# A gated cross-attention and FP4 feed-forward layer: two ScalarE steps moved ahead of other work, and four attention products put in one PSUM bank

## The chip, the cores and the metric

The kernel runs on one core of one Trainium2 chip. The metric is the time of one execution on the device in microseconds (us), the median of several runs; lower is better. The engines are named as in the profile: PE (TensorE, the matrix multiplier; PEld is its weight load), DVE (VectorE), ACT (ScalarE), POOL (GpSimd) and SP (SyncE, which here only issues DMAs). Each engine takes its own instructions in the order in which they are written and stops at a semaphore wait until another engine has counted far enough.

## The reference

What must be computed, for x of 8 x 512 x 512 and a context of 8 x 77 x 512, all in float32:

```python
def _L0_xattn_ref(k, v, q, Wk, Wv, bv, Wq, bq, Wo, bo):
    kp = jnp.einsum('bsd,ed->bse', k, Wk)
    vp = jnp.einsum('bsd,ed->bse', v, Wv) + bv
    qp = jnp.einsum('bsd,ed->bse', q, Wq) + bq
    scores = jnp.einsum('bqd,bkd->bqk', qp, kp) * scale
    probs = jax.nn.softmax(scores, axis=-1)
    ctx = jnp.einsum('bqk,bkd->bqd', probs, vp)
    return jnp.einsum('bqd,ed->bqe', ctx, Wo) + bo

def _L0_ffn_ref(x, w_gate, w_up, w_down):
    # fp4_linear quantizes both operands in blocks of 16 to the FP4 grid, then multiplies
    gate = fp4_linear(x, w_gate)          # 512 -> 1408
    y = fp4_linear(x, w_up)
    h = jax.nn.silu(gate) * y
    return fp4_linear(h, w_down)          # 1408 -> 512

x = x + jnp.tanh(g_xattn[0]) * _L0_xattn_ref(ctx, ctx, _layernorm(x), Wk, Wv, bv, Wq, bq, Wo, bo)
x = x + jnp.tanh(g_ffn[0]) * _L0_ffn_ref(_layernorm(x), w_gate, w_up, w_down)
```

## The kernel before

**Tiling.** x is worked on in 32 tiles (NT) of 128 rows, tile t; four tiles (TILES) are one batch b. The attention of batch b is spread over the four feed-forward steps of the batch ahead of it: in step t the helper attention_part(t, at) issues the pieces of batch b = t // 4 + 1, at named places ("a1" to "a4", "mid", "soft", "d soft").

**Order.** There is no scheduler. One program for each engine is written by hand: sync_program, pool_program, scalar_program, vector_program, tensor_program. Engines meet only through semaphores. The steps up to t = 3 are written out one by one; from t = 4 they stand in a loop. What comes first on an engine holds back all that stands behind it.

**The feed-forward step of a tile.** x_stats(t) on DVE and then on POOL (L603 to L608: add epsilon, negate the mean, power -1/2, multiply) makes the factors of the layer norm. x_apply(t) on ACT (L785) writes the normed row to xwork once the POOL part is done (semaphore x_rstd). DVE finds block maxima and divides (x_scales, x_divide), ACT squares (x_squares, L720), DVE rounds (x_round, L1182 and L1184), POOL multiplies by the scale (x_times, L570), ACT and DVE split the result in two float16 parts (x_high L883, x_low L1335), and a DMA transposes them to x_T (x_turn). PE multiplies: gate_up(t, c, m) is 12 matmuls (L1658) for column chunk c of gate (m = 0) or up (m = 1), where chunks 0 and 1 have 512 columns and chunk 2 has 384. ACT applies Silu (gate_silu, L877), DVE multiplies (hidden, L1351), h goes through the same quantizing as x (h_scales, h_divide, h_squares, h_round, h_times, h_high, h_low), and down(t, g) is 33 matmuls (L1782) for a tile.

**The down weights** are prepared while tiles 0 and 1 run, in four row groups r: down_turn(r) transposes into three banks (PE, L1664), down_high(r) is three casts on ACT (L761, semaphore d_hi) that write the high part, down_subtract(r) is three matmuls on PE (L1683) that each wait for their cast, and down_low(r) casts the rest (ACT, L767). On PE, down_subtract(1) stands between the two halves gate_up(1, 1, 0) and gate_up(1, 1, 1).

**The attention of batches 1 and 2.** att_turn(b, i) on PE (L1652) transposes the normed tile i, xn_copy(b, i) on ACT (L807) copies it to xnT, and att_scores(b, i) on PE waits for that copy (xn_sb). From batch 3 (CUT) on, DMAs transpose and these copies are not there. att_values(b, i) (PE, L1746 and L1747) multiplies probabilities and values into a bank, and values(b, i) on DVE (L1307) adds the bank to x; the two alternate by semaphores att_mm and x1_made. take(bank, freed_by) on PE waits until the last reader of that bank is done. In batch 2, att_values for i = 0 and 1 stands in step 6 among the down matmuls, for i = 2 and 3 in step 7 before and behind gate_up(7, 0, 1). In batch 2 the largest key is found as well: top_turn("k") on PE, power_of("k") on DVE (L1155 to L1159), and power_spread("k") on PE (L1698), which waits for DVE.

Of the kernel before, what the change touches and what calls it, by code (L numbers as in the profile page):

```python
# [61 lines left out]
def build(nc, x, ctx_kv, g_xattn, g_ffn, Wk, Wv, bv, Wq, bq, Wo, bo, w_gate, w_up, w_down, out):  # L62
# [20 lines left out]
    with ctx:  # L83
# [38 lines left out]
        def x_tile(t):  # L122
            s = (t // TILES) % SLOTS * SLOT + t % TILES * D
            return ring[:, s:s + D]
# [49 lines left out]
        CUT = 3  # L174
# [87 lines left out]
        def down_c(r):  # L262
            if r == 0:
                return xn1[:, :, :].rearrange("p i n -> p (i n)")[:, 0:HID // 2].bitcast(BF16)
            return h_c if r % 2 == 0 else h_v[:, 0:HID // 2].bitcast(BF16)
# [19 lines left out]
        def by_k(ap, k):  # L285
            return ap.rearrange("p (k n) -> p k n", k=k)
# [7 lines left out]
        for t in range(NT):  # L294
            b, s = t // TILES + 1, t % TILES
# [15 lines left out]
        def down_bank(r, g):  # L311
            return (4, 6, 7)[(r * NG + g) % 3]
# [9 lines left out]
            return KEYS_HALF * (1 if (b + 1) * KEYS <= HALF else 2)  # L322

        def value_bank(b, i):
            return (5, 4)[i % 2] if b == 0 else (5, 7, 4, 5)[i] if b == 1 else (5, 7, 5, 7)[i] if b < CUT else (7, 5)[i % 2]

        def rest_moves():
            return sum(len(list(value_moves(b))) for b in range(STACKED, NBATCH))
# [387 lines left out]
        def scalar_program(e):  # L716
            w = Waits(e)

            def square(c, v):
                return e.activation(c, v, ACT.Square, scale=ROOT)  # L720
# [21 lines left out]
            def down_squares(r):  # L742
                w.wait_ge(d_div, r + 1)
                if r == 0:
                    w.wait_ge(xn_turned, TILES)
                else:
                    w.wait_ge(gu_turned, 20)
                if r == 3:
                    w.wait_ge(d_neg, 2)
                square(down_c(r), down_raw[:, r, :]).then_inc(d_c, 1)  # L750
# [6 lines left out]
            def down_high(r):  # L757
                for g, ks in enumerate(GROUPS):
                    w.wait_ge(d_turned, r * NG + g + 1)
                    w.wait_ge(val_mm, CT)  # L760
                    e.copy(wd_hi[:, ks[0]:ks[-1] + 1, r * P:(r + 1) * P],  # L761
                           by_k(bank[down_bank(r, g)][:, 0:len(ks) * P], len(ks))).then_inc(d_hi, 1)
# [7 lines left out]
            def ln1_apply(b):  # L770
                w.wait_ge(ln1_rstd, b + 1)
                if b > 0:
                    w.wait_ge(xn_turned, TILES * b)
                if b == 1:
                    w.wait_ge(d_neg, 1)
                if b > STACKED:
                    w.wait_ge(att_mm, TILES * b)
                for i in range(TILES):
                    e.activation(xn1[:, i, :], x_tile(b * TILES + i), ACT.Identity, bias=shift1[:, i:i + 1], scale=rstd1[:, i:i + 1]).then_inc(xn_made, 1)

            def x_apply(t):
                w.wait_ge(x_rstd, t + 1)
                if t > 0:
                    w.wait_ge(xq_made, t)
                e.activation(x_v, x_tile(t), ACT.Identity, bias=shift2[:, :], scale=rstd2[:, :]).then_inc(x_norm, 1)  # L785
# [34 lines left out]
            def xn_apply(b, i):  # L820
                m = cut_tile(b, i)
                w.wait_ge(ln1_rstd, b + 1)
                if m >= 2:
                    w.wait_ge(xn_lo, m - 1)
                else:
                    w.wait_ge(xn_turned, TILES * CUT)
                    w.wait_ge(k_parts, KD)
                e.activation(xn1[:, 2 + i % 2, :], x_tile(b * TILES + i), ACT.Identity, bias=shift1[:, i:i + 1], scale=rstd1[:, i:i + 1]).then_inc(xn_made, 1)

            def xn_high(b, i):  # L830
                m = cut_tile(b, i)
                w.wait_ge(xn_made, b * TILES + i + 1)
                if i < 2:
                    w.wait_ge(att_mm, TILES * b)
                else:
                    w.wait_ge(*xn_there(b, i - 2))
                e.copy(xn_parts[i % 2][:, 0:D], xn1[:, 2 + i % 2, :]).then_inc(xn_hi, 1)

            def key_high(k):
                w.wait_ge(pow_ready, NTH["k"])  # L840
                w.wait_ge(xn_turned, TILES * CUT)
                w.wait_ge(v_stacked, VALUES_MOVED * (CUT - STACKED))
                if k == 3:
                    w.wait_ge(k_parts, 1)
                e.activation(key_work[k][:, 0:CUT_COLS], key_rest(k), ACT.Copy, scale=k_scale[:, :]).then_inc(k_hi, 1)

            def key_back(k):
                w.wait_ge(k_lo, k + 1)
                e.copy(key_rest(k).bitcast(F16).rearrange("p (b h n) -> p b h n", h=2, n=KEYS),
                       key_work[k].rearrange("p (h b n) -> p b h n", h=2, n=KEYS)).then_inc(k_parts, 1)  # L850
# [40 lines left out]
            def attention_part(t, at):  # L891
                b, s = t // TILES + 1, t % TILES
                if b >= NBATCH:
                    return
                if b == CUT - 1 and (s, at) == (2, "d soft"):
                    key_high(0)
                    key_high(1)
                elif b == CUT - 1 and (s, at) == (3, "a2"):
                    key_back(0)
                    key_back(1)  # L900
                    key_high(2)
                    key_high(3)
                elif b == CUT - 1 and (s, at) == (3, "a3"):
                    key_back(2)
                    key_back(3)
                elif b >= CUT and (s, at) == (0, "d apply"):
                    xn_apply(b, 0)
                    xn_apply(b, 1)
                    xn_high(b, 0)
                    xn_high(b, 1)  # L910
                elif b >= CUT and (s, at) == (1, "a1"):
                    xn_apply(b, 2)
                    xn_apply(b, 3)
                    xn_high(b, 2)
                    xn_high(b, 3)
                elif b >= CUT and (s, at) in ((0, "a3"), (0, "a4"), (1, "a2")):
                    return
                elif (s, at) == (0, "d apply"):
                    ln1_apply(b)
                elif (s, at) == (0, "a3"):  # L920
                    xn_copy(b, 0)
                elif (s, at) == (0, "a4"):
                    xn_copy(b, 1)
                elif (s, at) == (1, "a1"):
                    xn_copy(b, 2)
                elif (s, at) == (1, "a2"):
                    xn_copy(b, 3)
                elif (s, at) == (1, "d apply") and b >= STACKED:
                    value_high(b)
                elif (s, at) == (1, "d soft"):  # L930
                    exps(b)
                    if b >= STACKED:
                        prob_high(b)
                elif (s, at) == (2, "a1") and b < STACKED:
                    prob_copy(b)
# [113 lines left out]
            attention_part(1, "a1")  # L1049
            attention_part(1, "a2")  # L1050
            down_squares(3)
            down_high(1)
            x_apply(3)
            gate_silu(1, 1)
            down_low(1)
            down_high(2)
# [30 lines left out]
            for t in range(4, NT):  # L1087
                if t == 4:
                    h_squares(t - 1, 1)
                    gate_silu(t, 0)  # L1090
                    x_apply(t + 1)
                    h_high(t - 1, 0)
                    x_squares(t + 1)
                    x_high(t + 1)
                    gate_silu(t, 1)
                    h_high(t - 1, 1)
                else:
                    h_squares(t - 1, 1)
                    gate_silu(t, 0)
                    attention_part(t, "a1")  # L1100
                    h_high(t - 1, 0)
                    attention_part(t, "a2")
                    if t + 1 < NT:
                        x_squares(t + 1)
                    gate_silu(t, 1)
                    h_high(t - 1, 1)
                    if t % TILES == 0:
                        attention_part(t, "d apply")
                    if t + 1 < NT:
                        x_high(t + 1)  # L1110
                if t % TILES != 0 or t == 4:
                    attention_part(t, "d apply")
                gate_silu(t, 2)
                attention_part(t, "a3")
                h_squares(t, 0)
                attention_part(t, "a4")
                if t + 2 < NT:
                    x_apply(t + 2)
                attention_part(t, "d soft")
            h_squares(NT - 1, 1)  # L1120
            h_high(NT - 1, 0)
# [933 lines left out]
```

## Time and profile before

| | |
|---|---|
| Runs of the kernel before | 845.83, 843.76, 845.54 us; median 845.54 us |
| The profiled execution | 845.83 us, of which the span from the first to the last instruction is 844.0 us |
| Around the span | 1.8 us |
| Busy: PE, DVE | 834.8 us, 706.1 us |
| Busy: POOL, ACT | 400.5 us, 377.3 us |
| Granted clock of PE, mean | 0.997 of full |

The profile is of one execution. Timeline rows give the start in us from the span's start, the time of the instruction (or of several in a row, with xcount), engine, line and operation; in brackets stands how long the engine sat idle before it and what ended that. A matmul's time overlaps the next one's, so on PE the pace is read from start to start. The granted clock is 1.00 at 2.4 GHz and 0.50 at 1.2 GHz.

### The profile page before, as it was taken

To read this page: it belongs to the slowest core of one execution; us is meant where nothing else is said; L and a number is where in the kernel's file an instruction comes from. 1 tells how busy PE (TensorE), PEld (TensorE's weight loads), DVE (VectorE), ACT (ScalarE), POOL (GpSimd) and SP (SyncE) were. 2 spreads that over 40 slices of the span, in tenths; PEclk is the share of its full clock that TensorE was granted. 3 is DMA by queue.
4 is the path that set the end of the run, shared out by engine and by line. 5 is a ranking of instruction groups with operands and counts; after the bars stand their busy time and mean duration, and the time that the engine had idled before them with its cause. 6 is when DMAs were issued, how large, how long until landed. Compare 5 with 4: busy or idle time off the path is not lost.

```text
span 844.0 us, 11581 instructions
## 1 busy us (share of the span) xinstructions
PE 834.8 (99%) x4175; PEld 426.1 (50%) x4175; DVE 706.1 (84%) x1094; ACT 377.3 (45%) x669; POOL 400.5 (47%) x364
## 2 busy tenths in 40 slices
PE   9999999999998999999999999999999999999998
PEld 5566556544554445444544444445544454444443
DVE  5997989898989889888888888888897998877753
ACT  2666485643544544434453445335532454333320
POOL 4496437355544354446434544445354444444321
PEclk9999999999999999999999999999999999999999
DMA  9723020054324215432452254324432343222332
GB/s 317 278 70 118 18 61 14 14 119 109 72 59 122 60 28 116 114 68 55 104 134 60 60 110 97 96 60 85 87 81 59 71 93 77 54 57 51 62 63 72
DMA packets 170527, 72.69 MB, mean 86 GB/s; under 512 B 154227, under 2 KB 155621, under 8 KB 170471
## 3 DMA queue, kind: packets, MB, share of 16 engines
q1 hardware_dynamic: 170471, 71.97, 35.8%
q8 instruction: 33, 0.54, 0.3%
q14 instruction: 23, 0.19, 0.1%
HBM read 22.76 MB, written 8.39 MB: 37 GB/s over the span
## 4 chain that ended last, share of the span: by engine, by line
PE 62%; DVE 4%; issue 3%; POOL 1%; ACT 1%; DMA 1%; SPq 0%; POOLq 0%; ACTq 0%; DVEq 0%
PE banks L1658 39%; PE banks L1782 20%; PE banks L1721 1%; PE banks L1747 1%; PE banks L1746 1%; DVE arena L1182 1%; DVE arena L1184 1%; POOL arena L570 0%; DMA arena<-h_parts 0%; DMA x_T<-x_parts 0%; POOL rstd L597 0%; PE banks L1722 0%; DVE x_parts L1335 0%; DVE stats L1224 0%; DVE h_s L1131 0%
## 5 line engine op out<-in xcount | busy, mean ns | idle before, releaser
L1658 PE MATMUL banks<-wgu_hi,x_T 128*128 128x512 f16 (+1 forms) x1536 | 442.4, 362 | 0.1
L1658 PE MATMUL banks<-wgu_lo,x_T 128*128 128x512 f16 (+1 forms) x768 | 278.1, 362 | 0.0
L1782 PE MATMUL banks<-wd,arena 128*128 128x512 f16 x1056 | 233.8, 379 | 0.5 <-DMA arena<-h_parts 0.5
L1658 PEld LDWEIGHTS banks<-wgu_hi,x_T 128*128 128x128 f16 x1536 | 150.5, 98 | 154.7 <-issue 2.6
L1782 PEld LDWEIGHTS banks<-wd,arena 128*128 128x128 f16 x1056 | 102.9, 98 | 122.1 <-issue 0.9
L570 POOL TENSOR_TENSOR arena<-arena,h_r 128x1024 f32<-128x1024 f32 (+1 forms) x60 | 91.1, 1519 | 127.3 <-DVE h_r L1136 127.3
L570 POOL TENSOR_TENSOR arena<-arena,h_s 128x1024 f32<-128x1024 f32 x64 | 90.3, 1411 | 63.2 <-DVE arena L1184 45.2
L1658 PEld LDWEIGHTS banks<-wgu_lo,x_T 128*128 128x128 f16 x768 | 75.3, 98 | 76.8 <-issue 1.8
L570 POOL TENSOR_TENSOR xwork<-xwork,x_s 128x512 f32<-128x512 f32 x32 | 34.2, 1069 | 154.9 <-DVE xwork L1184 154.7
L1351 DVE SCALAR_TENSOR_TENSOR arena<-arena,scal,banks 128x512 f32<-128x512 f32 (+1 forms) x90 | 62.1, 690 | 34.6 <-PE banks L1658 30.5
L1182 DVE SCALAR_TENSOR_TENSOR arena<-arena 128x384 f32<-128x384 bf16 (+1 forms) x67 | 70.9, 1059 | 17.9 <-ACT arena L720 17.8
L877 ACT ACTIVATE arena<-banks,scal 128x512 f32<-128x512 f32 (+1 forms) x96 | 61.8, 644 | 49.8 <-PE banks L1658 49.7
L720 ACT ACTIVATE arena<-arena 128x384 bf16<-128x384 f32 (+1 forms) x67 | 54.2, 809 | 60.7 <-POOL arena L570 60.5
L785 ACT ACTIVATE xwork<-ring,shift,rstd 128x512 f32<-128x512 f32 x32 | 26.1, 814 | 120.4 <-POOL shift L608 120.4
L1184 DVE SCALAR_TENSOR_TENSOR arena<-arena 128x384 f32<-128x384 bf16 (+1 forms) x67 | 67.6, 1008 | 2.3
L570 POOL TENSOR_TENSOR arena<-arena,valo 128x1024 f32<-128x1024 f32 x22 | 49.4, 2263 | 29.5 <-DVE valo L1136 19.3
L1370 DVE TENSOR_TENSOR h_parts<-arena,h_parts 128x1024 f16<-128x1024 f32 x64 | 60.6, 950 | 2.1 <-ACT h_parts L889 2.0
L889 ACT CAST h_parts<-arena 128x1024 f16<-128x1024 f32 x64 | 49.2, 771 | 14.6 <-POOL arena L570 14.6
L1131 DVE TENSOR_REDUCE h_s<-arena 128x64 f32<-128x1024 f32 (+1 forms) x60 | 52.7, 878 | 0.5
L720 ACT ACTIVATE xwork<-xwork 128x512 bf16<-128x512 f32 x32 | 20.1, 628 | 61.7 <-DVE xwork L1327 61.7
L1375 DVE SCALAR_TENSOR_TENSOR ring<-banks,scal,ring 128x512 f32<-128x512 f32 x32 | 23.8, 744 | 28.5 <-PE banks L1782 28.4
L883 ACT CAST x_parts<-xwork 128x512 f16<-128x512 f32 x32 | 19.7, 617 | 44.4 <-POOL xwork L570 44.4
(175 smaller groups left out, 1009.1 us busy)
## 6 DMA issues: line engine op xcount, KB each, us to landing
ring<-in_x_dram SPq DMA_DIRECT2D x8, 1024.0 KB, 5.2
out_dram<-ring SPq DMA_DIRECT2D x32, 256.0 KB, 2.0
arena<-in_L_ffn_w_down_dram SPq DMA_DIRECT2D x4, 704.0 KB, 4.0
arena<-in_L_ffn_w_gate_dram SPq DMA_DIRECT2D x5, 512.0 KB, 9.7
arena<-in_L_ffn_w_up_dram SPq DMA_DIRECT2D x5, 512.0 KB, 10.4
ring<-in_L_xattn_Wk_dram SPq DMA_DIRECT2D x4, 256.0 KB, 6.2
ring<-in_L_xattn_Wq_dram SPq DMA_DIRECT2D x4, 256.0 KB, 6.8
wd<-in_ctx_dram SPq DMA_DIRECT2D x1, 1024.0 KB
```

Of the source, the lines that this page charges most:

```text
L570: return e.tensor_tensor(blocks(dst), blocks(src), spread(s), ALU.mult)
L720: return e.activation(c, v, ACT.Square, scale=ROOT)
L785: e.activation(x_v, x_tile(t), ACT.Identity, bias=shift2[:, :], scale=rstd2[:, :]).then_inc(x_norm, 1)
L877: e.activation(silu[par][:, 0:n], bank[par][:, 0:n], ACT.Silu, scale=p_gu).then_inc(silu_done, 1)
L889: e.copy(h_parts[:, PARTS[i]], h_q[:, PARTS[i]]).then_inc(h_hi[i], 1)
L1131: e.tensor_reduce(s, blocks(src), axis=AX_X, op=ALU.max, apply_absolute_value=True).then_inc(*step())
L1182: e.scalar_tensor_tensor(between, square, FLOOR, v, ALU.add, ALU.add).then_inc(*step())
L1184: return e.scalar_tensor_tensor(v, square, FLOOR, between, ALU.add, ALU.subtract)
L1351: e.scalar_tensor_tensor(h_of(t)[:, c0:c0 + n], silu[par][:, 0:n], h_fold, bank[2 + par][:, 0:n], ALU.mult, ALU.mult).then_inc(h_made, 1)
L1370: e.tensor_tensor(h_parts[:, lo], h_q[:, PARTS[i]], h_parts[:, PARTS[i]], ALU.subtract).then_inc(h_lo[i], 1)
L1658: ended = e.matmul(at, l, r, start=(i == 0), stop=(i == len(terms) - 1))
L1782: ended = e.matmul(down_ps(t)[:, :], l, r, start=(k == 0 and i == 0), stop=(k == KH - 1 and i == 2))
```

## The change

```diff
@@ value_bank: the PSUM bank of att_values(b, i) and values(b, i)
-            return (5, 4)[i % 2] if b == 0 else (5, 7, 4, 5)[i] if b == 1 else (5, 7, 5, 7)[i] if b < CUT else (7, 5)[i % 2]
+            return (5, 4)[i % 2] if b == 0 else (5, 7, 4, 5)[i] if b == 1 else 5 if b < CUT else (7, 5)[i % 2]
@@ scalar_program, written-out part
             attention_part(1, "a1")
             attention_part(1, "a2")
             down_squares(3)
+            x_apply(3)
             down_high(1)
-            x_apply(3)
             gate_silu(1, 1)
             down_low(1)
             down_high(2)
@@ scalar_program, loop for t in range(4, NT)
                 gate_silu(t, 2)
                 attention_part(t, "a3")
                 h_squares(t, 0)
-                attention_part(t, "a4")
                 if t + 2 < NT:
                     x_apply(t + 2)
+                attention_part(t, "a4")
                 attention_part(t, "d soft")
```

First, x_apply(3) stands before the three casts of down_high(1) instead of behind them. On ACT, in the written-out part (L785 is x_apply(3), the L761 rows are down_high(1), the L877 row is gate_silu(1, 1)):

```order
 L807 COPY xnT<-banks 128x512 [waits score_mm,xn_turned] x2
 L720 ACTIVATE arena<-arena 128x1408 [waits d_neg,d_div]
+L785 ACTIVATE xwork<-ring,shift,rstd 128x512 [waits x_rstd]
 L761 CAST wd<-banks 128x4x128 [waits d_turned] x2
 L761 CAST wd<-banks 128x3x128 [waits d_turned]
-L785 ACTIVATE xwork<-ring,shift,rstd 128x512 [waits x_rstd]
 L877 ACTIVATE arena<-banks,scal 128x512 [waits h_made,gate_mm]
 L767 CAST wd<-banks 128x4x128 [waits d_less] x2
```

The wait for x_rstd now stands ahead of the casts, and the casts behind it.

Second, in the loop x_apply(t + 2) stands before attention_part(t, "a4"). ACT has something at "a4" only for batch 2, which is t = 4, so that one pair changes places. On ACT at the end of step 4 (L785 is x_apply(6), the moved L807 is xn_copy(2, 1), the L796 and L720 rows are h_squares(4, 0) and (4, 1)):

```order
 L796 ACTIVATE h_s<-h_s 128x64 [waits h_rec0]
 L720 ACTIVATE arena<-arena 128x1024 [waits h_rounded0,h_div0]
+L785 ACTIVATE xwork<-ring,shift,rstd 128x512 [waits x_rstd]
 L807 COPY xnT<-banks 128x512 [waits score_mm,xn_turned]
-L785 ACTIVATE xwork<-ring,shift,rstd 128x512 [waits x_rstd]
 L796 ACTIVATE h_s<-h_s 128x24 [waits h_rec1]
 L720 ACTIVATE arena<-arena 128x384 [waits h_rounded1,h_div1]
```

The copy that att_scores(2, 1) waits for now stands behind a wait for POOL.

Third, the four products of batch 2 all go to bank 5 instead of banks 5, 7, 5, 7. On PE the order is the same, only waits differ. In step 6, among the down matmuls (L1782), at att_values(2, 1):

```order
 L1782 MATMUL banks<-wd,arena 128x512 [waits h_turned,x2_made]
 L1782 MATMUL banks<-wd,arena 128x512 x23
-L1746 MATMUL banks<-valo,xn 128x512 [waits pow_ready]
+L1746 MATMUL banks<-valo,xn 128x512 [waits x1_made]
 L1747 MATMUL banks<-valo,xn 128x512
 L1782 MATMUL banks<-wd,arena 128x512 x9
```

Each of the products i = 1, 2, 3 now waits (x1_made) until DVE has done values(2, i - 1), where before i = 2 waited for values(2, 0) and i = 3 for values(2, 1). DVE, POOL and SP have the same instructions in the same order.

## Rows read from the trace of the kernel before

**Rows 1.** The page, part 1: busy us, share of the span, instructions.

```profile
PE 834.8 (99%) x4175; PEld 426.1 (50%) x4175; DVE 706.1 (84%) x1094; ACT 377.3 (45%) x669; POOL 400.5 (47%) x364
```

**Rows 2.** Windows: stretch, length, busy of each engine, PE's clock, DMA share, GB/s.

```profile
250.00:270.00 20.00, 17.84 (x83) 8.60 (x82) 17.11 (x38) 11.11 (x20) 6.32 (x5) 0.91 0.41 108
...
290.00:330.00 40.00, 39.85 (x207) 19.16 (x206) 35.34 (x59) 19.22 (x34) 20.68 (x21) 1.00 0.42 88
```

**Rows 3.** Timeline of ACT around down_high(1), x_apply(3) and gate_silu(1, 1).

```profile
136.72 1.46 ACT L761 CAST wd<-banks 128x512 f16<-128x512 f32 x3 [0.23 <-PE banks L1664]
140.43 0.81 ACT L785 ACTIVATE xwork<-ring,shift,rstd 128x512 f32<-128x512 f32 x1 [2.26 <-POOL shift L608]
141.15 0.67 ACT L877 ACTIVATE arena<-banks,scal 128x512 f32<-128x512 f32 x1
```

**Rows 4.** Timeline of PE at down_subtract(1) and what follows it.

```profile
139.88 0.76 PE L1683 MATMUL banks<-wd,neg_ident 128*128 128x512 f16 x3
140.47 0.38 PE L1658 MATMUL banks<-wgu_hi,x_T 128*128 128x512 f16 x1
```

**Rows 5.** Timeline of POOL: first and last of x_stats(2), then of x_stats(3).

```profile
119.12 0.23 POOL L603 TENSOR_SCALAR mv<-mv 128x1 f32<-128x1 f32 x1
...
120.37 0.19 POOL L608 TENSOR_TENSOR shift<-shift,rstd 128x1 f32<-128x1 f32 x1
...
135.16 0.55 POOL L603 TENSOR_SCALAR mv<-mv 128x1 f32<-128x1 f32 x1
...
139.32 1.08 POOL L608 TENSOR_TENSOR shift<-shift,rstd 128x1 f32<-128x1 f32 x1
```

**Rows 6.** Timelines: down_turn(3) on PE, down_high(3) on ACT, h_round(0, 0) on DVE.

```profile
149.60 1.36 PE L1664 MATMUL banks<-ident,arena 128*128 128x128 f32 x11
...
150.24 1.46 ACT L761 CAST wd<-banks 128x512 f16<-128x512 f32 x3 [1.06 <-PE banks L1664]
...
155.24 1.22 DVE L1182 SCALAR_TENSOR_TENSOR arena<-arena 128x1024 f32<-128x1024 bf16 x1 [1.84 <-ACT arena L720]
```

**Rows 7.** Timeline of ACT: xn_copy(2, 1), x_apply(6), xn_copy(2, 3), x_squares(6).

```profile
223.94 0.59 ACT L807 COPY xnT<-banks 128x512 f32<-128x512 f32 x1 [0.33 <-PE banks L1652]
227.66 0.81 ACT L785 ACTIVATE xwork<-ring,shift,rstd 128x512 f32<-128x512 f32 x1 [3.13 <-POOL shift L608]
...
231.80 0.59 ACT L807 COPY xnT<-banks 128x512 f32<-128x512 f32 x1 [0.81 <-PE banks L1652]
...
234.68 0.63 ACT L720 ACTIVATE xwork<-xwork 128x512 bf16<-128x512 f32 x1 [1.42 <-DVE xwork L1327]
```

**Rows 8.** Timeline of PE: att_scores(2, 1), then top_turn("v").

```profile
226.33 1.01 PE L1658 MATMUL banks<-keyq,xnT 128*128 128x77 f32 x8
...
230.21 0.23 PE L1691 MATMUL banks<-ident,scal 77*1 77x77 f32 x1
```

**Rows 9.** Timeline of DVE: power_of("v") and x_round(6).

```profile
233.48 0.22 DVE L1155 TENSOR_REDUCE scal<-banks 1x1 f32<-1x77 f32 x1
...
235.72 0.67 DVE L1182 SCALAR_TENSOR_TENSOR xwork<-xwork 128x512 f32<-128x512 bf16 x1
```

**Rows 10.** Timeline of PE at power_spread("k").

```profile
259.27 0.49 PE L1698 MATMUL banks<-scal,ones 1*128 1x1 f32 x2 [2.16 <-DVE scal L1159]
```

**Rows 11.** The chain that ended last, in order of time: start, us, what.

```profile
259.76 5.50 PE banks L1658 x24
...
265.69 5.18 PE banks L1782 x24
...
278.87 0.22 PE banks L1746
...
313.73 3.17 DMA x_T<-x_parts
...
323.19 9.08 PE banks L1658 x48
```

**Rows 12.** Timeline of DVE: values(2, 2).

```profile
278.38 0.65 DVE L1307 SCALAR_TENSOR_TENSOR ring<-banks,rden,ring 128x512 f32<-128x512 f32 x1
```

## The prediction

> **What bounds the kernel now.** I read the page's busy times first. PE is busy 99% of the span [rows 1], so what the change can win or lose is time in which PE stands still or runs at the lower clock. The timeline of PE and the windows show where that is. Between the start-up and the tail there is one stretch that matters: at 257 to 263 us. PE was done at 257.1 and waited 2.16 us for DVE's largest key before power_spread("k") at 259.27 [rows 10]. Behind that wait the granted clock fell: over 250 to 270 it averages 0.91 [rows 2], and 24 matmuls of 384 columns took 5.50 us in the chain. At full clock 24 of 512 and 24 of 384 columns take 9.08 us together and 24 of 512 take 5.18, so 24 of 384 take 3.90 [rows 11]. The fall to 1.2 GHz cost 5.50 - 3.90 = 1.6 us. After that PE idles 0.15 us in 290 to 330 [rows 2], where it waits for the transposed x_T whose DMA starts at 313.73 [rows 11]. From there to the tail PE does not stop. So up to about 317 us PE and the loop of DVE, ACT and POOL run neck and neck, and whatever delay is there at 317 stays in the time to the end. Nothing in the change touches the code behind that.
>
> **Edit 1: x_apply(3) ahead of down_high(1).** Before, the three casts of down_high(1) ran on ACT at 136.72 for 1.46 us, then ACT idled 2.26 us until POOL's factors let x_apply(3) start at 140.43, and gate_silu followed at 141.15, 0.72 later [rows 3]. POOL's instructions do not change, so x_apply(3) still starts at 140.43: nothing is won on it, and its reader on DVE comes only after 150 us. The casts now start where the silu started, at 141.15, and end at 141.15 + 1.46 = 142.6. PE wants them at 139.88, for down_subtract(1) [rows 4]. Its three matmuls each wait for a cast; the last can start at about 142.65 and takes 0.2. The next gate_up matmul, 140.47 before [rows 4], starts at about 142.9. **Stall 1 is 2.4 us.** Queued behind it on PE is everything, the transposes of down_turn(2) and (3) too.
>
> Does the loop of DVE, ACT and POOL hide it? ACT's down_high(3) at 150.24 had waited for PE's down_turn(3) of 149.60; behind it stand on ACT the exponentials of batch 1 and the square that h_round(0, 0) on DVE waited 1.84 us for, until 155.24 [rows 6]. That is one unbroken line from PE over ACT to DVE, so DVE too comes 2.4 us later from 155 on. I then followed DVE's idle times up to 259: each is ended by ACT or by POOL, which in turn waited for DVE. None waits for anything that stays in place. I take the whole 2.4 us to the end.
>
> **Edit 2: x_apply(6) ahead of xn_copy(2, 1).** Before, the copy ran at 223.94 and x_apply(6) waited 3.13 us for POOL until 227.66 [rows 7]. Now the copy starts 0.72 us after x_apply(6), at 228.38, and with its 0.59 us ends at 228.97. att_scores(2, 1) on PE ran at 226.33 [rows 8] and can now run at about 229.0. **Stall 2 is 2.7 us**, counted from where stall 1 has put both engines. Here part of it is covered. PE used to arrive at power_spread("k") at 257.1 and wait until 259.27 for DVE [rows 10]. Now it arrives at 257.1 + 2.7 = 259.8, no longer waits, and the 1.6 us of lower clock behind that wait fall away.
>
> What happens on DVE depends on the clock behind stall 2. A wait of 2.16 us was followed by the fall that cost 1.6 [rows 10, 11]; stall 2 is longer, so a fall behind it is more likely than not. If the clock stays, top_turn("v") moves from 230.21 [rows 8] to 232.9, before power_of("v") at 233.48 [rows 9]; xn_copy(2, 3) moves from 231.80 to 234.5, and the square behind it from 234.68 to 235.1 [rows 7], ending with its 0.63 us at 235.7, just when x_round(6) wants it at 235.72 [rows 9]. DVE loses nothing. If the clock falls, all that PE does there comes 1.6 later still: xn_copy(2, 3) at 231.80 + 4.3 = 236.1, the square 0.6 behind it at 236.7 and done at 237.3, so x_round(6) comes at 237.3 instead of 235.72 and DVE is 1.6 us late. No later idle time of DVE gives this back, for the reason above.
>
> **Edit 3: four products in bank 5.** The product i = 3 now waits until DVE has done values(2, 2). That ran at 278.38 for 0.65 us, to 279.03 [rows 12]; the product ran at 278.87 [rows 11]. By the old times this would be 0.2 us. But PE comes to it faster now. From power_spread("k") to that product PE took 278.87 - 259.27 = 19.6 us, 1.6 of them clock, so 18.0 now. With the clock kept at stall 2, PE is there at 259.8 + 18.0 = 277.8 and waits until 279.1: the gain of edit 2 is taken away, and what is left is 279.1 - 278.87 = +0.2 us. With the clock fallen, PE is there at 259.8 + 1.6 + 18.0 = 279.4, DVE is done at 279.03 + 1.6 = 280.6, and what is left is 280.7 - 278.87 = **+1.8 us**. The products i = 1 and 2 wait for values that DVE finished more than 1 us ahead; they cost nothing. The bank 7 that is left free has no other user there.
>
> **The sum**, against the profiled execution of 845.83 us (844.0 of span and 1.8 around it): stall 1 costs 2.4, edits 2 and 3 together 0.2 to 1.8. The clock behind stall 1 is the other open term. The trace has no stall of that shape: PE stands still 1.7 us, then runs three short matmuls 0.5 us apart. The nearest rows are the 2.16 us wait with a fall behind it, 1.6 us, and the 0.15 us wait in 290 to 330 with none [rows 2, 10, 11]; so 0 to 1.6, and I take 0, because this stall is broken up, and keep 1.6 for the range. The forecast is 2.4 + 1.8 = +4.2, 850.0 on the profiled execution, which lies 0.3 above the median of the runs: **849.7 us**. A fall behind stall 1 alone gives the same, 2.4 + 1.6 + 0.2 = +4.2.
>
> The Trainium skill (TensorE: Matmul & The Clock Gate, section HAM oscillation) names only idle gaps longer than both stalls here as what lowers the clock. By that rule there would be no fall, as in the first rival below. The trace speaks against it, since the clock fell behind a wait of 2.16 us.
>
> **Rivals.**
>
> *No fall at either stall.* 2.4 + 0.2 = +2.6, 848.1 us. For it: stall 1 is broken up, and there is only one fall in the trace to judge by. Against it: that fall came behind a shorter wait than stall 2.
>
> *A fall at both.* 2.4 + 1.6 + 1.8 = +5.8, 851.3 us.
>
> *POOL gets through earlier, and the change is not slower.* x_stats(3) on POOL took from 135.16 to 140.40, 5.2 us for four tiny instructions; the same four of x_stats(2) took from 119.12 to 120.56, 1.4 us [rows 5]. The long ones end just as DVE's long roundings of down weights end. If POOL slipped in ahead of DVE, x_apply(3) would start at 136.6, the casts would end at 138.8, before PE's 139.88 [rows 4], and stall 1 would be gone. It decides from an x_apply(3) at or before 137.7 on. Left are 0.2 to 1.8: 845.7 to 847.3 us. Against it: up to that point nothing on DVE or POOL moves, so the same meeting should come out the same.
>
> The Trainium skill (SBUF — State Buffer, section SBUF: two separate sides) says that DVE and POOL share one pair of ports as a lock which whoever starts first holds for a whole instruction; by that rule a small shift of phase could give this rival's time. The four POOL rows agree with a lock, but do not say how stable the order is.
>
> *DVE catches up.* If some wait of DVE that I took as internal has another cause, stall 1 delays PE alone and is partly eaten by the 2.16 us. PE then reaches the product i = 3 at 277.8 + 2.4 = 280.2 and no longer waits: 280.2 - 278.87 = +1.3, 846.8 us, or 848.4 with a fall.
>
> **How the numbers follow.** A measurement of this kernel can tell about 0.3% from no change, 2.5 us: under 843.0 is faster, over 848.1 slower. One fall, the forecast: 0.38. No fall: 0.22, on the edge of slower, half to each side. Both: 0.13. POOL gets through: 0.11. DVE catches up: 0.08, mostly within. A further fall behind the wait in edit 3, or DVE and POOL meeting more often: 0.05, up to 853. Faster: 0.03, for what I do not see, since all that can be won is the wait and the fall of clock at 257 to 263, 3.8 us, and DVE holds PE there and again at 279. Slower 0.38 + 0.11 + 0.13 + 0.05 + 0.02 = 0.69, within 0.28, faster 0.03. The range runs from 846.7, in the middle of the not-slower rivals, to 851.7, just above both falls.
>
> **What the profile after would show.** Right: PE idle about 1.7 us ahead of L1683 near 140, ended by ACT's cast L761, and L1683 spread over a microsecond; x_apply(3) still at 140.4; h_round(0, 0) on DVE near 157.6; PE idle 2.6 us ahead of att_scores(2, 1) near 231, ended by ACT L807; no wait at power_spread("k"); PE idle 1 us or more at the product i = 3, ended by DVE L1307; a window at clock 0.5 behind the second stall. Wrong: x_apply(3) well before 140; DVE at 155.2 as before; a wait at power_spread("k") that is still there, which would mean DVE is slower than I think, and the time above 852.

## The result

| | median, us | runs | ratio to before, 95% interval |
|---|---|---|---|
| before | 845.54 | 5 runs, 843.34 to 845.83 | |
| changed | 849.9 | 5 runs, 848.83 to 850.18 | 1.0058 [1.0042, 1.0075] |

The change makes the kernel 0.6% slower, 4.4 us by the medians; 849.7 was forecast. The profiled execution of the changed kernel took 850.62 us (span 848.8).

The waits of PE in the changed kernel (for whom, us in total, times, longest):

```profile
PE banks L1658 <- ACT xnT L807: 2.5, 1, 2.5
PE banks L1683 <- ACT wd L761: 1.8, 1, 1.8
...
PE banks L1746 <- DVE ring L1307: 1.4, 1, 1.4
```

These are stall 2, stall 1 and the wait of the fourth product, in that order; the wait at power_spread("k") of [rows 10] is gone. **Stall 1**, on ACT and then on PE:

```profile
140.18 0.81 ACT L785 ACTIVATE xwork<-ring,shift,rstd 128x512 f32<-128x512 f32 x1 [3.95 <-POOL shift L608]
140.90 1.43 ACT L761 CAST wd<-banks 128x512 f16<-128x512 f32 x3
```
```profile
141.52 1.20 PE L1683 MATMUL banks<-wd,neg_ident 128*128 128x512 f16 x3 [1.76 <-ACT wd L761]
142.56 0.46 PE L1658 MATMUL banks<-wgu_hi,x_T 128*128 128x512 f16 x1
...
147.68 1.36 PE L1664 MATMUL banks<-ident,arena 128*128 128x128 f32 x11
```

All times of this trace lie 0.25 us lower than those of before from the start-up on (x_apply(3) at 140.18 against 140.43 [rows 3]). The start-up differs by up to 1.2 us among all the traces (the first L1658 matmul starts between 22.43 and 23.60), so times of two traces are compared only after such a shift. With that, gate_up(1, 1, 1) starts 142.56 + 0.25 - 140.47 = 2.3 us later than in [rows 4]. The windows after it (stretch, length, busy times, then the clock) show what came on top:

```profile
142.00:144.00 2.00, 2.00 (x6) 0.76 (x7) 2.00 (x1) 2.00 (x5) 0.69 (x1) 0.68 0.00 0
144.00:146.00 2.00, 2.00 (x6) 0.76 (x5) 1.96 (x4) 0.26 (x1) 1.76 (x1) 0.50 0.00 0
146.00:148.00 2.00, 2.00 (x16) 1.55 (x14) 1.97 (x4) 0.00 (x0) 1.28 (x2) 0.97 0.00 0
```

The clock fell to 1.2 GHz behind stall 1: 2 x (0.32 + 0.50 + 0.03) = 1.7 us of full-clock work lost. DVE carries both: h_round(0, 0), at 155.24 before [rows 6], stands at 159.02, which is 4.0 us later with the 0.25.

```profile
159.02 1.23 DVE L1182 SCALAR_TENSOR_TENSOR arena<-arena 128x1024 f32<-128x1024 bf16 x1 [4.75 <-ACT arena L720]
```

**Stall 2 and the fourth product**, on PE (power_spread("k") between them has no bracket, so no wait):

```profile
232.82 1.12 PE L1658 MATMUL banks<-keyq,xnT 128*128 128x77 f32 x8 [2.55 <-ACT xnT L807]
...
263.63 0.38 PE L1698 MATMUL banks<-scal,ones 1*128 1x1 f32 x2
...
283.07 0.39 PE L1746 MATMUL banks<-valo,xn 128*128 128x512 f16 x1 [1.45 <-DVE ring L1307]
```

The clock kept 1.00 behind both. att_scores(2, 1) is 232.82 + 0.25 - 226.33 = 6.7 us later than in [rows 8]: 4.0 from stall 1 and its clock, and the 2.7 us that were forecast for stall 2. In the timeline of before the fourth product stands at 278.70 (the 278.87 of [rows 11] is where its piece of the chain starts, after the matmuls ahead of it):

```profile
278.70 0.38 PE L1746 MATMUL banks<-valo,xn 128*128 128x512 f16 x1
```

So it is 283.07 + 0.25 - 278.70 = 4.6 us later: 4.0 from stall 1 and its clock, and 0.6 from edits 2 and 3, of which 0.3 is left once PE is past the x_T wait of before. In the chain the last full tile of down matmuls but one starts at 801.45, where it started at 797.37 before:

```profile
801.45 7.14 PE banks L1782 x33
```

That is 4.3 us with the 0.25. The rest of the span's 4.8 us is in the tail, where the issue of the last transposes on SP took 1.97 us; this row of before had 1.24.

```profile
832.81 1.97 SPq L484
```
```profile
828.73 1.24 SPq L484
```

### The profile page after: what moved, and what is told of

It reads as the page before. It is cut to its first block, busy times and chain, and to the rows that moved or that the text cites. A ratio compares the mean times of both kernels' runs of the same rounds, so it can differ in the third digit from the quotient of the medians.

```text
span 848.8 us, 11581 instructions
## 1 busy us (share of the span) xinstructions
PE 835.3 (98%) x4175; PEld 425.7 (50%) x4175; DVE 706.2 (83%) x1094; ACT 377.0 (44%) x669; POOL 398.7 (47%) x364
## 4 chain that ended last, share of the span: by engine, by line
PE 63%; DVE 3%; issue 2%; ACT 1%; POOL 1%; DMA 0%; SPq 0%; DVEq 0%; POOLq 0%; ACTq 0%
PE banks L1658 40%; PE banks L1782 21%; PE banks L1721 1%; PE banks L1746 1%; PE banks L1747 1%; DVE arena L1184 1%; DVE arena L1182 0%; POOL arena L570 0%; DVE h_parts L1370 0%; DMA arena<-h_parts 0%; PE banks L1722 0%; DVE h_s L1131 0%; SPq L484 0%; DVE ring L1375 0%; DVE arena L1351 0%
## 5 line engine op out<-in xcount | busy, mean ns | idle before, releaser
L1658 PE MATMUL banks<-wgu_hi,x_T 128*128 128x512 f16 (+1 forms) x1536 | 442.4, 362 | 0.0
L1658 PE MATMUL banks<-wgu_lo,x_T 128*128 128x512 f16 (+1 forms) x768 | 278.2, 362 | 0.0
L1782 PE MATMUL banks<-wd,arena 128*128 128x512 f16 x1056 | 233.8, 379 | 1.1 <-DMA arena<-h_parts 1.1
L1658 PEld LDWEIGHTS banks<-wgu_hi,x_T 128*128 128x128 f16 x1536 | 150.6, 98 | 154.2 <-issue 2.5
L1782 PEld LDWEIGHTS banks<-wd,arena 128*128 128x128 f16 x1056 | 103.0, 98 | 122.8 <-DVE ring L1375 1.6
L1658 PEld LDWEIGHTS banks<-wgu_lo,x_T 128*128 128x128 f16 x768 | 75.2, 98 | 77.1 <-issue 2.1
L877 ACT ACTIVATE arena<-banks,scal 128x512 f32<-128x512 f32 (+1 forms) x96 | 61.9, 645 | 49.7 <-PE banks L1658 49.6
L720 ACT ACTIVATE arena<-arena 128x384 bf16<-128x384 f32 (+1 forms) x67 | 54.2, 809 | 61.8 <-POOL arena L570 61.6
L785 ACT ACTIVATE xwork<-ring,shift,rstd 128x512 f32<-128x512 f32 x32 | 26.1, 814 | 122.6 <-POOL shift L608 122.6
L720 ACT ACTIVATE xwork<-xwork 128x512 bf16<-128x512 f32 x32 | 20.1, 628 | 60.3 <-DVE xwork L1327 60.3
```

The costliest lines, as they stand in the source:

```text
L877: e.activation(silu[par][:, 0:n], bank[par][:, 0:n], ACT.Silu, scale=p_gu).then_inc(silu_done, 1)
L1658: ended = e.matmul(at, l, r, start=(i == 0), stop=(i == len(terms) - 1))
L1782: ended = e.matmul(down_ps(t)[:, :], l, r, start=(k == 0 and i == 0), stop=(k == KH - 1 and i == 2))
```

## The times fall into groups

The runs come in groups, and the mean granted clock of each run tells them apart. Of the twelve traced executions the five with a fall of the clock in mid-kernel read 0.995 to 0.998, and the seven without one read 0.999 or 1.000. For the runs that were not traced the mean is all there is: it does not say where the clock fell. In the three comparisons of the experiments the kernel before ran 65 times:

| kernel | clock 0.999 or 1.000, us | clock 0.998 or lower, us |
|---|---|---|
| before | 31 runs, 24 at 843.4 to 844.5, seven at 845.1 to 846.1 | 34 runs, 845.3 to 846.6 |
| changed | 1 run, 848.83 | 5 runs, 849.8 to 850.6 |
| e1_first | 2 runs, 846.2 and 847.5 | 4 runs, 848.3 to 850.1 |
| e23 | 6 runs, 845.6 to 845.9 | 6 runs: two 847.6 and 848.0, four 849.3 to 850.1 |
| e12 | 2 runs, 845.7 and 848.4 | 7 runs, 848.8 to 850.5 |
| e2_second | 6 runs, 843.9 to 845.7 | 6 runs, 847.4 to 848.2 |
| e3_banks | 6 runs, 845.1 to 846.2 | 5 runs, 845.8 to 846.5 |

So a fall comes in about half of the runs of before; the one trace of it has the fall behind the 2.16 us wait of [rows 10]. Its median, 844.2 to 845.7 us in three comparisons, depends on how many. The traces show behind which waits of PE the clock fell:

| wait of PE | clock kept in the trace of | clock fell in the trace of, time lost |
|---|---|---|
| stall 1, 1.7 to 1.8 us, then three short matmuls | e1_first, e12, a_soft | changed, 1.7 us |
| stall 2, 2.5 us | changed, e23, a_soft | e2_second, 1.7 us; e12, 3.4 us |
| power_spread("k"), 2.2 us | e1_first, e3_banks | before and e1_sub_late, 1.7 us each |
| fourth product, 1.4 to 1.9 us | changed, e23, e3_banks | none |

The time lost is the length of each 2 us window times what its clock lacks to 1, summed. What each kernel in the tables changes is told below, and each is read by groups as well as by its ratio.

## Experiments

### Each edit by itself

**The first edit alone** (e1_first):

```diff
             down_squares(3)
+            x_apply(3)
             down_high(1)
-            x_apply(3)
             gate_silu(1, 1)
```

> Only the first edit: x_apply(3) ahead of down_high(1). Theory (one unbroken line PE, ACT, DVE): PE idles 1.7 us ahead of L1683 near 140, h_round(0, 0) on DVE starts 4.0 us later than 155.24 with a fall of the clock behind the stall (2.4 + 1.6), and PE still waits about 2.2 us at power_spread("k"), since DVE is as late as PE. Time +4.0 us with the fall, +2.4 without. Rival (the stall delays PE alone, DVE catches up): the wait at power_spread("k") is gone and the time is +0.3 us (4.0 - 2.16 - 1.6).

Measured: 849.11 us, ratio 1.0041 [1.0025, 1.0056]. The profiled run is one without any fall. PE, and DVE's h_round(0, 0):

```profile
141.17 1.21 PE L1683 MATMUL banks<-wd,neg_ident 128*128 128x512 f16 x3 [1.75 <-ACT wd L761]
...
261.08 0.35 PE L1698 MATMUL banks<-scal,ones 1*128 1x1 f32 x2 [2.22 <-DVE scal L1159]
```
```profile
156.99 1.23 DVE L1182 SCALAR_TENSOR_TENSOR arena<-arena 128x1024 f32<-128x1024 bf16 x1 [4.19 <-ACT arena L720]
```

PE still waits 2.22 us at power_spread("k"), although it comes there 2.4 us later. DVE is as late as PE: this trace lies 0.60 us lower from the start-up on (x_apply(3) at 139.83), so h_round(0, 0) is 156.99 + 0.60 - 155.24 = 2.35 us late. The stall is not absorbed: the rival in which DVE catches up has fallen. The two runs without a fall took 846.2, 2.3 us above the 843.9 of before without falls, and 847.5; of the four with one, three took 849.9 to 850.1 and one 848.3.

**The first edit with cover** (e1_sub_late). On PE, down_subtract(1) goes behind the next 12 matmuls:

```diff
             gate_up(1, 1, 0)
-            down_subtract(1)
             gate_up(1, 1, 1)
+            down_subtract(1)
             attention_part(1, "a3")
```

> The first edit, and on PE down_subtract(1) behind gate_up(1, 1, 1) instead of ahead of it, so that 2.6 us of matmuls cover the late casts. Theory (the cost of the first edit is the PE stall, and nothing else): PE idles under 0.3 us at L1683, perhaps 0.5 at down_turn(2) for down_low(1), no fall of the clock; +0.2 to +0.8 us. Rival (what costs is ACT's later order itself, down_high, down_low and the silu pushed back): +2 us or more.

Measured: 845.76 us, ratio 1.0001 [0.9992, 1.0009]. ACT and PE:

```profile
140.34 0.81 ACT L785 ACTIVATE xwork<-ring,shift,rstd 128x512 f32<-128x512 f32 x1 [3.95 <-POOL shift L608]
141.06 1.43 ACT L761 CAST wd<-banks 128x512 f16<-128x512 f32 x3
```
```profile
142.37 0.76 PE L1683 MATMUL banks<-wd,neg_ident 128*128 128x512 f16 x3
```

ACT's order is that of e1_first, x_apply(3) waits the same 3.95 us, the casts still come at 141, and PE does not wait. Of the cost of the first edit nothing is left that the interval, -0.7 to +0.8 us, can tell from zero. What it cost was the PE stall and the clock behind it. The late down_subtract(1) was not run without the first edit; before, PE did not wait there [rows 4], so there was no wait for it to win.

**The third edit alone** (e3_banks):

```diff
-            return (5, 4)[i % 2] if b == 0 else (5, 7, 4, 5)[i] if b == 1 else (5, 7, 5, 7)[i] if b < CUT else (7, 5)[i % 2]
+            return (5, 4)[i % 2] if b == 0 else (5, 7, 4, 5)[i] if b == 1 else 5 if b < CUT else (7, 5)[i % 2]
```

> The third edit alone: the four products of batch 2 in bank 5. Theory: PE waits 0.2 us for values(2, 2) at the fourth product when the clock has fallen at 257 to 263, and up to 1.8 us when it has not, which takes away what a run without the fall had won: runs with the fall stay at 845.8, runs without it come from 843.9 to 845.5. Rival (the bank is free in time, no cost): both groups stay, 845.8 and 843.9.

Measured: 845.79 us, ratio 1.0008 [0.9999, 1.0017]. By groups: with a fall 845.8 to 846.5, as before; without one five of six runs at 845.1 to 845.6 instead of 843.9. The profiled run had no fall, and PE waited twice:

```profile
258.79 0.35 PE L1698 MATMUL banks<-scal,ones 1*128 1x1 f32 x2 [2.22 <-DVE scal L1159]
278.61 0.39 PE L1746 MATMUL banks<-valo,xn 128*128 128x512 f16 x1 [1.86 <-DVE ring L1307]
```

The bank takes away the 1.6 us that most runs without a fall had won, and nothing from a run with it. (Of the nine runs of before without a fall in this comparison, five took 843.6 to 844.5 and four 845.1 to 846.1.)

**The second edit alone** (e2_second), x_apply(t + 2) ahead of "a4" as in the change, banks as before:

```diff
-                attention_part(t, "a4")
                 if t + 2 < NT:
                     x_apply(t + 2)
+                attention_part(t, "a4")
```

> The second edit alone, banks 5, 7, 5, 7 as before. Theory (DVE holds the time at the next steps): PE does not wait at power_spread("k") nor at the fourth product, is 1.2 us ahead of before when it reaches it, and loses that again when it waits for DVE's next results by 317; 0.0 us, or up to +1.6 if the clock falls behind the stall. Rival (PE alone sets the time): -1.2 us.

Measured: 846.54 us, ratio 1.0015 [1.0004, 1.0026]. The profiled run is one in which the clock fell behind stall 2, the case that the forecast had taken as the likeliest. A window behind the stall (the three from 228 to 234 read 0.92, 0.50 and 0.73, 1.7 us lost), and what DVE waited for:

```profile
230.00:232.00 2.00, 2.00 (x7) 0.90 (x6) 1.93 (x5) 1.40 (x2) 0.61 (x1) 0.50 0.34 131
```
```profile
234.58 0.23 DVE L1155 TENSOR_REDUCE scal<-banks 1x1 f32<-1x77 f32 x1 [1.36 <-PE banks L1691]
...
237.17 0.69 DVE L1182 SCALAR_TENSOR_TENSOR xwork<-xwork 128x512 f32<-128x512 bf16 x1 [0.29 <-ACT xwork L720]
```

DVE idles 1.36 + 0.29 = 1.65 us there, and with this trace's shift of 0.35 us (x_apply(3) at 140.07) x_round(6) starts 237.17 + 0.35 - 235.72 = 1.8 us later than in [rows 9], where the prediction had worked out 1.6. Runs with the fall took 847.4 to 848.2, about 2 us over before with its own fall (845.8). Without a fall they took 845.2 to 845.7, one 843.9.

**The second and third** (e23):

> The second and third edit without the first. Theory: PE idles 2.6 us ahead of att_scores(2, 1), does not wait at power_spread("k"), and waits 1.3 to 1.5 us for values(2, 2) at the fourth product of batch 2; +0.2 us without a fall of the clock behind the first of these, +1.8 with it. Rival (the three edits need each other, and the cost of the changed kernel is spread over them): +2 us or more without a fall.

Measured: 846.77 us, ratio 1.0027 [1.0013, 1.0041]. Its six runs without a fall took 845.6 to 845.9, which is before with its fall and 1.9 us over most runs of before without one, and the profiled one, of these, has

```profile
278.71 0.39 PE L1746 MATMUL banks<-valo,xn 128*128 128x512 f16 x1 [1.44 <-DVE ring L1307]
```

and no other long wait but stall 2. The four runs at clock 0.995 or 0.996 took 849.3 to 850.1, 2 us above the two at 0.997. No trace of such a run was taken. A second fall behind the 1.4 us wait is one reading. One fall of twice the length behind stall 2 is another, and the trace of e12, below, has it; e2_second, which has no wait at the fourth product, read 0.996 in three runs too. Which it was is open.

**The first and second** (e12), with the old banks:

> The first and second edit with the old banks 5, 7, 5, 7: what the wait of 1.4 us at the fourth product costs in the changed kernel. Theory (DVE would hold PE a little later anyway): 0.2 us less than the changed kernel, 849.7. Rival (the wait costs its full length where x_T(9) comes early, as it does with POOL's power at 1.41 us): 848.5.

Measured: 849.67 us, ratio 1.0047 [1.0032, 1.0061], against 1.0058 of the change. The two ratios are 0.9 us apart and the intervals overlap, so these runs decide neither for the 0.2 us that was expected nor for the rival's 1.4. One run, without a fall, took 845.65 us, 3.2 below the fastest of the changed kernel; no trace shows it. In the trace the fourth product does not wait, and PE waits later instead:

```profile
321.53 0.38 PE L1658 MATMUL banks<-wgu_hi,x_T 128*128 128x512 f16 x1 [1.33 <-DMA x_T<-x_parts]
```

This trace has no fall behind stall 1, but a long one behind stall 2:

```profile
228.00:230.00 2.00, 0.00 (x0) 0.00 (x0) 2.00 (x1) 1.04 (x2) 1.84 (x4) 0.95 0.00 0
230.00:232.00 2.00, 1.71 (x8) 1.71 (x9) 2.00 (x3) 1.35 (x4) 0.81 (x1) 0.50 0.00 0
232.00:234.00 2.00, 2.00 (x9) 1.31 (x9) 1.90 (x5) 0.83 (x2) 0.84 (x1) 0.50 0.34 131
234.00:236.00 2.00, 2.00 (x6) 0.67 (x5) 0.86 (x2) 0.70 (x1) 0.00 (x0) 0.50 0.00 0
236.00:238.00 2.00, 2.00 (x13) 1.14 (x11) 0.34 (x2) 0.00 (x0) 0.00 (x0) 0.84 0.00 0
```

That is 2 x (0.05 + 0.50 + 0.50 + 0.50 + 0.16) = 3.4 us lost in one fall, twice what the other four traced falls cost.

### What holds PE between 317 and 322

The wait for x_T(9) shows in some traces (0.15 us in before, 1.35 in e2_second, 1.33 in e12) and not in others. The long case goes with one POOL instruction of the layer norm of batch 3 (L597, the power -1/2). In before and in the changed kernel, beside the DVE instruction that runs then:

```profile
305.04 3.15 POOL L597 TENSOR_TENSOR rstd<-mv,neg_half 128x4 f32<-128x4 f32 x1
```
```profile
304.86 0.69 DVE L1327 TENSOR_TENSOR xwork<-xwork,x_r 128x512 f32<-128x512 f32 x1
```
```profile
309.21 1.41 POOL L597 TENSOR_TENSOR rstd<-mv,neg_half 128x4 f32<-128x4 f32 x1
```
```profile
309.03 0.68 DVE L1327 TENSOR_TENSOR xwork<-xwork,x_r 128x512 f32<-128x512 f32 x1
```

The two start 0.18 us apart in both traces, and once POOL takes 3.15 us and once 1.41. It took 3.15 in before, e2_second, e1_sub_late and e12, and 1.41 in the changed kernel, e1_first, e3_banks, s1_soft, s2_klate, s3_both and a_soft. Where it takes 3.15, x_T(9) comes 1.6 us later by DVE's instructions (from hidden(8, 1) to the end of x_low(9) 5.8 us in before, 4.2 in the changed kernel). Nearly all of this is the length of x_low(9) itself. In before POOL's multiply started ahead of it, in the changed kernel behind it:

```profile
311.22 1.93 POOL L570 TENSOR_TENSOR arena<-arena,h_r 128x1024 f32<-128x1024 f32 x1 [1.17 <-DVE h_r L1136]
```
```profile
311.60 2.10 DVE L1335 TENSOR_TENSOR x_parts<-xwork,x_parts 128x512 f16<-128x512 f32 x1 [0.46 <-ACT x_parts L883]
```
```profile
315.66 0.63 DVE L1335 TENSOR_TENSOR x_parts<-xwork,x_parts 128x512 f16<-128x512 f32 x1
```
```profile
315.82 2.25 POOL L570 TENSOR_TENSOR arena<-arena,h_r 128x1024 f32<-128x1024 f32 x1 [2.50 <-DVE h_r L1136]
```

x_low(9) ended 0.55 us behind POOL's multiply and took 2.10 us, or started 0.16 us ahead of it and took 0.63. The same two lengths go with the same two orders in all twelve traces, and with 3.15 and 1.41 of the power. In e23 the power took 3.15 too, and there PE did not wait for x_T(9), since the fourth product had held it already. This may be why runs of before without a fall form two groups, 843.9 and 845.5 us; no such run was traced, the start-up alone differs by up to 1.2 us, and what decides the length of the power is open.

### A version that is faster than both

In before ACT holds DVE ahead of 259: DVE idles 2.24 us at prob_low(2), behind the exponentials, which stand on ACT behind x_apply(7).

```profile
253.53 0.48 DVE L1284 SCALAR_TENSOR_TENSOR xn<-prob,xn 128x308 f16<-128x308 f32 x1 [2.24 <-ACT xn L859]
```

The first experiment puts them ahead of it (s1_soft); the second leaves them and moves power_spread("k") on PE 3.9 us of matmuls later (s2_klate); s3_both does both.

```diff
                 attention_part(t, "a4")
+                if t == 5:
+                    attention_part(t, "d soft")
                 if t + 2 < NT:
                     x_apply(t + 2)
-                attention_part(t, "d soft")
+                if not (t == 5):
+                    attention_part(t, "d soft")
```
```diff
-                attention_part(t, "mid")
+                if t != 6:
+                    attention_part(t, "mid")
                 gate_up(t, 2, 0)
                 gate_up(t, 2, 1)
+                if t == 6:
+                    attention_part(t, "mid")
```

> The kernel before with one ACT pair of step 5 in the other order: the exponentials and the high part of batch 2's probabilities ("d soft") ahead of x_apply(7), which waits for POOL until 249.5, while the exponentials' maxima are there at 247.0. Theory (DVE, held 2.24 us at 253.5 by ACT, is what holds PE at power_spread("k") and at x_T(9)): power_of("k") comes 2.2 us earlier, PE waits under 0.3 us there, no fall of the clock behind it, and x_T(9) is there in time whichever way POOL's power and DVE fall out at 305; 845.7 - 2.2 - 1.6 = 841.9 us in all runs. Rival (another wait takes its place, x_apply(7) being 0.7 us later): 843.7 or more.

> The kernel before with power_spread("k") on PE 3.9 us of matmuls later, behind gate_up(6, 2, 1), where its number is long there. Theory from the traces so far: no wait and no fall of the clock at 257 to 263, PE 3.8 us ahead of before at 263, but DVE is not a bit earlier, so PE waits at 317 for x_T(9): about 1.7 to 3.5 us, by POOL's power at 305 taking 1.41 or 3.15 us; 843.7 to 845.5 us, clock 1.000 or a fall behind the new wait. Rival (PE alone sets the time): 841.9.

> Both: "d soft" ahead of x_apply(7) on ACT and power_spread("k") later on PE. Theory: the same 841.9 us as the first alone, within 0.3, since the wait is gone already. Rival (the first alone still waits at power_spread("k") or leaves a fall): lower than the first alone by 1 us or more.

Measured: s1_soft 841.47 us, ratio 0.9959 [0.9946, 0.9973], all five runs between 841.0 and 842.3; s2_klate 844.68, 1.0005 [0.9993, 1.0016], ten runs at 843.8 to 846.1 without a fall and two at 847.3 and 848.0 with one; s3_both 842.41, 0.9969 [0.9956, 0.9983], which these runs don't tell apart from s1_soft. ACT in s1_soft:

```profile
243.45 1.28 ACT L812 ACT_TABLE_LOAD   x1
246.42 1.11 ACT L812 ACTIVATE prob<-prob,neg_top 128x77 f32<-128x77 f32 x4 [1.69 <-DVE neg_top L1249]
247.56 0.72 ACT L859 ACTIVATE xn<-prob 128x616 f16<-128x616 f32 x1
248.86 0.81 ACT L785 ACTIVATE xwork<-ring,shift,rstd 128x512 f32<-128x512 f32 x1 [0.58 <-POOL shift L608]
```

DVE no longer waits for ACT at prob_low(2), PE waits neither at power_spread("k") nor for x_T(9), and in these five runs the clock did not fall below a mean of 0.999. In s2_klate PE does not wait at power_spread("k") but, with DVE as late as ever, three times later on:

```profile
269.85 0.38 PE L1658 MATMUL banks<-wgu_hi,x_T 128*128 128x512 f16 x1 [0.29 <-DMA x_T<-x_parts]
305.14 0.34 PE L1658 MATMUL banks<-wgu_hi,x_T 128*128 128x384 f16 x1 [0.57 <-DVE arena L1351]
315.46 0.38 PE L1658 MATMUL banks<-wgu_hi,x_T 128*128 128x512 f16 x1 [1.07 <-DMA x_T<-x_parts]
```

Moving PE's wait alone won nothing in the median; shortening what DVE waits for wins both the wait and the clock.

**The changed kernel with the same ACT pair turned** (a_soft) tells whether the changed kernel's two stalls are covered by anything else:

> The changed kernel with "d soft" ahead of x_apply(7) on ACT, so that DVE is 2.2 us earlier from step 6 on. Theory: the waits at the fourth product and at x_T(9) are gone and PE alone sets the time; both stalls now count in full against the 841.5 us of s1_soft: 841.5 + 2.4 + 2.7 = 846.6 without falls of the clock, 848.2 with one, 849.8 with two. Rival (stall 2 stays covered by DVE, which is held by something else): 841.5 + 2.4 = 843.9, 845.5 with a fall.

Measured: 848.87 us, ratio 1.0040 [1.0025, 1.0054]; the run without a fall, which is the profiled one, took 846.70 us, where 846.6 was expected (841.5 + 2.4 + 2.7), three at clock 0.998 took 848.8 to 849.0, and one at 0.996 took 849.4. With DVE early, both stalls count in full and no other wait is left in this stretch:

```profile
141.67 1.21 PE L1686 MATMUL banks<-wd,neg_ident 128*128 128x512 f16 x3 [1.74 <-ACT wd L761]
```
```profile
231.28 1.12 PE L1661 MATMUL banks<-keyq,xnT 128*128 128x77 f32 x8 [2.54 <-ACT xnT L807]
```

## Why the prediction was right, and where not

**Stall 1, 2.4 us, kept to the end: right.** x_apply(3) did not move, L1683 was spread over 1.2 us, and h_round(0, 0) was 4.0 us late with the clock. e1_first shows the persistence (the wait at power_spread("k") unchanged) and e1_sub_late shows that the stall is the cause.

**The clock behind stall 1: the wrong choice of two.** The forecast took 0 of a range of 0 to 1.6 "because this stall is broken up". It fell there in the profiled run of the change, and kept 1.00 behind the same stall in the traces of e1_first, e12 and a_soft. In 4 of 6 runs of e1_first the mean clock shows a fall, though in those runs the wait at power_spread("k") may carry it. How often stall 1 brings a fall is open, and so is which stall brought the falls of the other four changed runs at 0.998. The trace of before could not tell: with one execution, one fall says nothing of how often it comes. The price, 1.6 us against 1.7 measured, was right here; the 3.4 us fall of e12 was in no branch.

**Edits 2 and 3: the mechanism right, the branch another.** Stall 2 was 2.55 us of idling and 2.7 of delay, as forecast; the wait at power_spread("k") was gone, and the fourth product waited 1.45 us. The forecast counted +1.8 with a fall behind stall 2, the profiled run had none there and so +0.6 at the product, 0.3 to the end, where +0.2 had been worked out. Part of that gap is a reading: the prediction took the product's start from the chain, 278.87, and not from the timeline, 278.70. The two wrong branches offset each other: 2.4 + 1.6 + 0.2 = 4.2 was the second way to the same time that the prediction names. That 849.7 met 849.9 is partly luck of this kind. What the +1.8 branch says of DVE is seen in e2_second, where DVE was late by 1.8 us.

**What the prediction missed.** It took before's trace as the kernel before. That trace had both of its accidents, the fall behind the 2.16 us wait and the 3.15 us power on POOL. "No fall: 848.1" was 0.7 us low for the one run without a fall, 848.83. And the argument that DVE holds PE again at 279 and 317 holds only in part: in e2_second, with POOL's power long, PE waits 1.35 us for x_T(9), while in s2_klate, with it short, PE waits only 0.29 + 0.57 + 1.07 = 1.9 us although it was to be 3.8 ahead. By this a run of before without the fall keeps its 1.6 us where the power is short and loses it where it is long; that is worked out and not seen in a trace.

**POOL slips in early, the rival that was not slower:** it did not happen. The four instructions of x_stats(3) took from 134.90 to 140.15 in the changed kernel, 5.2 us as in [rows 5], and the same in all the other traces. That the long ones end with DVE's roundings was read too broadly: in before two of three do (at 137.22 and 137.15, at 140.40 and 140.35), and the third ends at 139.24, 0.4 us behind a rounding.

```profile
134.90 0.55 POOL L603 TENSOR_SCALAR mv<-mv 128x1 f32<-128x1 f32 x1
...
139.07 1.08 POOL L608 TENSOR_TENSOR shift<-shift,rstd 128x1 f32<-128x1 f32 x1
```

**The rule on the clock.** The Trainium skill (TensorE: Matmul & The Clock Gate, section HAM oscillation) names only longer gaps than those here. Here falls came behind a 2.16 us wait, behind waits of 2.5 us, and behind a 1.76 us wait that three short matmuls followed, so the measurement decides against it.

## What to carry to other kernels

On an engine that takes its instructions in order, look at what stands behind a wait before moving the wait forward: here an instruction that waits 2 to 4 us for POOL was put ahead of short copies that PE needed at once, and nothing that read it came sooner. Where PE waits for DVE, look for what DVE waits for: turning one pair on ACT won 0.4%, and moving PE's own wait won nothing. Where a short PE wait can bring the clock down, one trace is one draw: group the runs by their mean clock, and take the start-up out, before a difference of 0.3% is explained.

## What the runs showed of the hardware

A wait of about 2.2 us of PE was followed by a stretch at 1.2 GHz in two of four traces, and by the mean clock roughly half of the runs of one and the same program (34 of 65) had a fall. Four of the five traced falls cost 1.7 us and one, behind a 2.5 us wait, 3.4. One small POOL instruction took 1.41 or 3.15 us at the same distance of 0.18 us from the DVE instruction beside it, and one DVE subtraction, x_low(9), took 0.63 us where it started 0.16 us ahead of a POOL multiply and 2.10 us where it started 0.38 us behind one. And the load of ACT's exponential table ran at 243.45 in s1_soft, 3 us ahead of the exponentials themselves, which still waited for DVE: where an instruction of another function waits, the 1.28 us of its table load can pass during the wait.
